# A graph network and a mixture of experts on one core: products up with all three parts in the same columns, GELU out of PSUM, and four reorderings

## The chip, the cores and the metric

The kernel runs on one NeuronCore of a Trainium2 chip. The metric is the time on the device in microseconds (us), the median of the runs shown. A profile is one execution recorded by the hardware; its times count from the start of the profiled span. The engines are TensorE (PE; PEld is its loading of weights), VectorE (DVE), ScalarE (ACT), GpSimd (POOL) and SyncE (SP), which issues plain DMAs.

## What is computed

A graph network on 1250 nodes of 512 features is added to its input, and then a mixture of 8 experts is added to that: each of the first 512 rows goes, normalised, through the two experts drawn for it, weighted.

```
x = x + gnn(layernorm(x))                 # two layers over 41250 edges, three decoder products
xf = layernorm(x)[:512]                   # the tokens of the experts
order = argsort(expert_indices.reshape(-1)); token_ids = order // 2
xg = xf[token_ids]
for e in range(8):
    h = gelu(xg @ w1[e], approximate=False)     # 512 -> 256
    y = where(bin_ids == e, h @ w2[e], y)       # 256 -> 512
x = x + zeros.at[token_ids].add(w * y)
```

(The edges are 20000 drawn pairs in both directions and a loop at each node. In the last line the sum has as many rows as there are tokens.)

## The kernel before

**Stages.** The adjacency matrix is built by TensorE from one-hot rows that VectorE makes (line 752). The two layers of the network are products of it with the features, cut into two or three bf16 parts (lines 1681, 1810, 1819). A decoder of three FP32 products follows (lines 1775, 1783, 1793), 128 rows a chunk for the last, ten chunks c. `sum_rows` (line 1082) adds a chunk's result to x. The first four chunks are the tokens; they are normalised and stored to `x2_rows` in HBM, from which each expert's rows are gathered.

**Routing.** Beside the first layer VectorE finds for each token and expert the slot it gets. An expert has 128 + 32 slots (`SLOTS` = 160, `MORE` = 32); the last 32 of four experts (a team, `TEAM` = 4) are gathered and scattered together, as `tail`. The scatter-adds of one token's two results must not be under way together. So an assignment is marked `late` (must be among an expert's last 32, the tails) or `early` (must be among the first 128), or is free. Late is a pair of neighbouring experts' second, early its first, and early is also the lower of two experts of one team. Before, lines 921 to 928 make these marks. `load` (lines 969 to 974) holds the fullest lists against their limits and chooses the sparse or a dense path; here the sparse one is taken, by all engines at the branch `sparse != 0`. `scale_sum1` (line 984) then scales the first layer's sums.

**Experts.** All products of the experts have both operands in two parts, hi and lo, each FP32 rounded to fp32r and its rest; of the four cross products the one of both rests is left out. Per expert e:

- TensorE transposes the gathered rows (`transpose_gathered`, 1859; `transpose_tails`, 1869). ScalarE takes the hi part out of PSUM (1406, 1411), VectorE the rest (1112, 1116).
- `up_slots` makes two halves m of the 256 hidden features, each in a bank of its own, 2 + m. Four products (line 1886) of w1's hi part with x's hi and lo lying side by side fill 320 columns, four (line 1889) of w1's rest with x's hi add to the first 160.
- ScalarE copies the right 160 columns out (`keep_part`, 1426), VectorE adds the left ones (`sum_hidden`, 1127). Only then may TensorE write the banks again. ScalarE makes the GELU (1444), a hi copy (1448) and the tails' GELU (1450); VectorE the rest (1150).
- `down_slots` (1848) gives 512 columns; VectorE scales them by the weight (`keep_results`, 1135). `down_tails` (1911) and `keep_tails` (1433) do the same for the tails of a team.
- ScalarE rounds the weights of expert e + 3 (`first_parts`, 1418), VectorE takes their rests (`up_rest`, 1060; `down_rest`, 1063). The weights of experts 0 and 1 are rounded by GpSimd (658), their rests are taken between additions (`weights_rest`, 1057).

TensorE's order is: up 0, then for each e up e + 1, transposes e + 2, down e; after experts 3 and 7 the tails' product.

**Scatter-adds.** GpSimd issues them (672) in the order of experts, the tails of team 0 after expert 3's, those of team 1 last. That of expert e waits until that of expert e − 2 has landed, and from expert 4 on until the first tails' has:

```
                    if e >= 2:
                        pool.wait_ge(s_added[e % 2], 16 * (e // 2))
                    if e >= TEAM:
                        pool.wait_ge(s_added_more, 16 * (e // TEAM))
```

The second tails' scatter-add waits for expert 6's. A scatter-add adds 128 rows to `out`; a slot that is free has a row of its own behind the tokens.

## Time and profile before

| | us |
|---|---|
| median of 3 runs | 169.47 |
| lowest, highest | 169.32, 170.09 |
| the profiled execution | 169.9 |
| its span | 168.1 |
| TensorE busy in it | 144.9 |
| VectorE busy in it | 130.9 |
| ScalarE, GpSimd busy in it | 90.9, 41.4 |

The granted clock of TensorE is full until its last product. The timeline puts like instructions in a row together: its start, its length, engine, line, operation, tiles and count, and in brackets how long the engine had been idle before it and who released it. A row of products is longer than the distance to the next row, since the end of one product overlaps the start of the next; the distances between starts tell what a group costs. Where two products are recorded for one FP32 product, the count is double.

### The profile page before, as it was taken

To read this page: it belongs to the slowest core of one execution; us is meant where nothing else is said; L and a number is where in the kernel's file an instruction comes from. 1 tells how busy PE (TensorE), PEld (TensorE's weight loads), DVE (VectorE), ACT (ScalarE), POOL (GpSimd) and SP (SyncE) were. 2 spreads that over 40 slices of the span, in tenths; PEclk is the share of its full clock that TensorE was granted. 3 is DMA by queue.
4 is the path that set the end of the run, shared out by engine and by line. 5 is a ranking of instruction groups with operands and counts; after the bars stand their busy time and mean duration, and the time that the engine had idled before them with its cause. 6 is when DMAs were issued, how large, how long until landed. Compare 5 with 4: busy or idle time off the path is not lost.

```text
span 168.1 us, 3574 instructions
## 1 busy us (share of the span) xinstructions
PE 144.9 (86%) x1146; PEld 99.4 (59%) x1149; DVE 130.9 (78%) x317; ACT 90.9 (54%) x224; POOL 41.4 (25%) x57
## 2 busy tenths in 40 slices
PE   2968899999999999989999999899968999987500
PEld 1446677888788757546735444445957886875100
DVE  1899999999999789996469388399759999895100
ACT  3278777777788784013314506903588896653100
POOL 8300000000000000000000900078204877618550
PEclk9999999999999999999999999999999999999975
DMA  4999999994000000000000003335890986543874
GB/s 90 324 350 254 349 375 368 366 364 166 4 0 4 6 0 6 0 0 4 0 0 0 4 0 125 125 101 159 275 388 15 191 170 101 95 66 48 107 106 62
DMA packets 15355, 21.72 MB, mean 129 GB/s; under 512 B 2942, under 2 KB 7808, under 8 KB 15332
## 3 DMA queue, kind: packets, MB, share of 16 engines
q1 hardware_dynamic: 12994, 16.02, 28.7%
q0 software_dynamic: 2240, 5.24, 17.6%
q8 instruction: 13, 0.21, 0.5%
q10 hardware_dynamic: 98, 0.17, 0.3%
q14 instruction: 10, 0.08, 0.2%
HBM read 15.19 MB, written 6.23 MB: 127 GB/s over the span
## 4 chain that ended last, share of the span: by engine, by line
PE 45%; DVE 26%; ACT 9%; issue 7%; DMA 6%; POOL 2%; POOLq 1%; DVEq 0%; ACTq 0%
DVE ring L752 11%; PE bank L1560 9%; PE bank L1793 7%; DMA out<-at,to_i 6%; PE bank L1535 4%; PE bank L1886 3%; PE bank L1681 3%; PE bank L1889 2%; PE bank L1481 2%; PE bank L1819 2%; PE bank L1525 2%; DVE stats L1088 2%; PE bank L1848 2%; DVE x_sb L1082 2%; DVE ring L900 2%
## 5 line engine op out<-in xcount | busy, mean ns | idle before, releaser
L1560 PE MATMUL bank<-ring 128*128 128x110 bf16 x324 | 30.0, 222 | 3.9 <-DVE ring L752 2.7
L752 DVE TENSOR_TENSOR ring<-iota_slots,lo 128x1024 bf16<-128x1024 f16 (+1 forms) x41 | 27.4, 669 | 0.0
L1560 PEld LDWEIGHTS bank<-ring 128*128 128x128 bf16 x324 | 19.7, 98 | 11.9 <-issue 5.9
L658 POOL CAST at_r<-ew 128x1024 fp32r<-128x1024 f32 x4 | 4.6, 1183 | 83.6 <-PE bank L1810 83.6
L1266 ACT CAST at<-bank 128x400 f32 (+1 forms) x41 | 20.6, 503 | 7.5 <-PE bank L1566 6.7
L752 DVE TENSOR_TENSOR ring<-iota_dst,key 128x880 bf16<-128x880 f16 (+1 forms) x41 | 24.4, 594 | 0.0
L672 POOL DMA_INDIRECT out<-at,to_i x10 | 19.0, 1898 | 19.8 <-DVE at L1135 8.8
L1793 PE MATMUL bank<-wd3t_sb,at 128*128 128x512 f32 x40 | 17.9, 598 | 0.7 <-ACT at L1365 0.7
L1681 PE MATMUL bank<-at,ring 128*128 128x512 bf16 (+1 forms) x89 | 16.7, 343 | 0.1
L661 POOL DMA_INDIRECT ring<-x_rows,from_i x10 | 12.7, 1269 | 15.5 <-DMA x_rows<-at 12.8
L1886 PE MATMUL bank<-xnt_r,at_r 128*128 128x320 f32 x64 | 12.9, 323 | 2.9 <-DVE ring L1127 2.6
L1793 PEld LDWEIGHTS bank<-wd3t_sb,at 128*128 128x128 f32 x40 | 7.4, 190 | 10.0 <-issue 8.1
L1886 PEld LDWEIGHTS bank<-xnt_r,at_r 128*128 128x128 f32 x64 | 9.5, 189 | 6.0 <-issue 5.1
L1848 PE MATMUL bank<-at_r 128*128 128x512 f32 x32 | 11.9, 414 | 1.2 <-DVE at_r L1150 1.2
L1681 PEld LDWEIGHTS bank<-at,ring 128*128 128x128 bf16 x90 | 8.7, 98 | 7.0
L1418 ACT CAST at_r<-ew 128x1024 fp32r<-128x1024 f32 x12 | 11.9, 1037 | 0.0
L1535 PE MATMUL bank<-w1c,xnt 128*128 128x129 f32 x80 | 11.4, 284 | 0.0
L1082 DVE TENSOR_TENSOR x_sb<-x_sb,bank 128x512 f32<-128x512 f32 x10 | 6.8, 684 | 5.8 <-PE bank L1793 5.7
L1535 PEld LDWEIGHTS bank<-w1c,xnt 128*128 128x128 f32 x80 | 9.8, 191 | 0.1
L1889 PE MATMUL bank<-xnt_r,ew_r 128*128 128x160 f32 x64 | 9.2, 266 | 0.0
L1406 ACT CAST xnt_r<-bank 128x256 fp32r<-128x256 f32 x16 | 5.1, 372 | 7.3 <-PE bank L1859 7.3
L1889 PEld LDWEIGHTS bank<-xnt_r,ew_r 128*128 128x128 f32 x64 | 8.9, 190 | 0.0
(226 smaller groups left out, 267.0 us busy)
## 6 DMA issues: line engine op xcount, KB each, us to landing
ew<-in_w SPq DMA_DIRECT2D x16, 512.0 KB, 9.5
x_sb<-in_x SPq DMA_DIRECT2D x9, 256.0 KB, 5.0
out<-x_sb SPq DMA_DIRECT2D x9, 256.0 KB, 4.4
wd3t_sb<-in_Wd3T SPq DMA_DIRECT2D x1, 512.0 KB, 5.3
x_rows<-xn SPq DMA_DIRECT2D x1, 512.0 KB, 2.8
x_rows<-at SPq DMA_DIRECT2D x1, 512.0 KB, 2.8
w1t_sb<-in_W1T SPq DMA_DIRECT2D x1, 256.0 KB, 4.5
bd_sb<-in_bd SPq DMA_DIRECT2D x1, 256.0 KB, 4.5
```

What stands on the lines that cost most here:

```text
L661: nc.gpsimd.indirect_dma_start(to, None, x2_rows, bass.IndirectOffsetOnAxis(from_i[:, i:i + 1].bitcast(mybir.dt.uint32), 0)).then_inc(gath ...
L672: nc.gpsimd.indirect_dma_start(out[0:T + 3 * P, :], bass.IndirectOffsetOnAxis(to_i[:, i:i + 1].bitcast(mybir.dt.uint32), 0), of, None, com ...
L752: last = v.tensor_tensor(hot[:, slot, 0:tiles].rearrange("p t (n a) -> p t n a", a=2), lanes[:, 0:n].rearrange("p (n a) -> p n a", a=2).un ...
L1266: nc.scalar.copy(at[:, :, bass.ds(column, wide)], bank[j][:, 0:CH * wide].rearrange("p (c n) -> p c n", c=CH)).then_inc(s_placed, 1)
L1418: nc.scalar.copy(hi, w).then_inc(s_whi_act, 1)
L1535: last = mm(bank[6][:, 0:HID + 1], xnt[:, k, c * P:(c + 1) * P], w1c[:, k], start=(k == 0), stop=(k == KD - 1))
L1560: last = mm(to, hot_src[:, j, t], hot_dst[:, j, t], start=(t == 0 and not ends), stop=(first and t == tiles - 1), skip_group_check=not ends)
L1681: last = mm(bank[4 + i][:, 0:n], parts[k][:, s], at[:, s, a:a + n], start=(k == 0 and s == 0), stop=(k == last_k and s == CH - 1))
L1793: last = mm(bank[4 + c % 4][:, 0:D], y2t[:, k, c * P:(c + 1) * P], wd3t_sb[:, k], start=(k == 0), stop=(k == 1))
L1848: last = mm(acc, lhs(a, k), rhs(b, k), start=(i == 0), stop=(i == len(passes) - 1))
L1886: mm(acc[:, 0:2 * SLOTS], w1_hi[:, k, m * P:(m + 1) * P], xg_t[:, e % 2, k].rearrange("p h t -> p (h t)"), start=(k == 0), stop=False)
L1889: last = mm(acc[:, 0:SLOTS], w1_lo[:, e, k, m * P:(m + 1) * P], xg_t[:, e % 2, k, 0], start=False, stop=(k == KD - 1))
```

## The change

Six things are changed.

1. **Products up**: the hi and lo parts of x now meet w1's hi part in two products of 160 columns, one after the other, that add into the same columns as the third part. Both halves m lie in one bank, and experts take the banks 2 and 3 in turn. TensorE waits for the GELU of expert e − 2 instead of for `sum_hidden`.
2. **GELU from PSUM**: `keep_part` and `sum_hidden` are gone, and ScalarE's GELU reads the bank.
3. **Additions**: with `FREE` = 6 only the scatter-adds of experts 6 and 7 wait for the first tails'. For that, in team 0 the lower of a pair is also early where the other expert is 4 or 5, so the marks are made in another way, with one step fewer.
4. **Weights**: the rests of experts 0 and 1 are taken one by one after chunks 3 to 6, and that of expert 2's w1 before chunk 8.
5. **Decoder**: the first activation of the second span goes ahead of the second square root, and `decode3` waits for each of its two input halves by itself.
6. **Scaling**: the first `scale_sum1` goes ahead of the comparison of loads.

```diff
@@ add_to_tokens
-                    if e >= TEAM:
+                    if e >= FREE:            # FREE = TEAM + 2
                         pool.wait_ge(s_added_more, 16 * (e // TEAM))
@@ routing marks
-            for i, k in enumerate((0, 1, 0)):
-                v.scalar_tensor_tensor(in_turn[:, :, i], gif[:, :, 1 - k], 1.0, gif[:, :, k], ALU.add, ALU.is_equal)
+            for k in range(TOPK):
+                v.scalar_tensor_tensor(in_turn[:, :, k], gif[:, :, 1 - k], 1.0, gif[:, :, k], ALU.add, ALU.is_equal)
...
-            late, early = in_turn[:, :, 0:TOPK], in_turn[:, :, 1:TOPK + 1]
-            v.tensor_scalar(team[:, :, :], gif[:, :, :], float(TEAM), None, ALU.is_ge)
+            v.tensor_scalar(team[:, :, :], gif[:, :, :], float(TEAM), float(NE - FREE), ALU.is_ge, ALU.mult)
             for k in range(TOPK):
                 last = v.tensor_tensor(below[:, :, k], gif[:, :, k], gif[:, :, 1 - k], ALU.is_lt)
             link(last)
-            link(v.tensor_tensor(one_team[:, :], team[:, :, 0], team[:, :, 1], ALU.is_equal))
-            link(v.tensor_tensor(below[:, :, :], below[:, :, :], one_team[:, :].unsqueeze(2).to_broadcast([P, TC, TOPK]), ALU.mult))
-            link(v.tensor_tensor(below[:, :, :], below[:, :, :], early, ALU.max))
-            early = below[:, :, :]
+            for k in range(TOPK):
+                last = v.scalar_tensor_tensor(team[:, :, k], team[:, :, k], float(FREE), gif[:, :, 1 - k], ALU.add, ALU.is_gt)
+            link(last)
+            link(v.tensor_tensor(below[:, :, :], below[:, :, :], team[:, :, :], ALU.mult))
+            late, early = in_turn[:, :, 0:TOPK], below[:, :, :]
@@ VectorE, weights and chunks
-            for c in range(CH - 1):
+            for c in range(CH - 3):
                 sum_rows(c)
...
-                if c == TC + 1:
-                    weights_rest(0)
-                if c == TC + 3:
-                    weights_rest(1)
+                if c >= TC - 1:
+                    weight_rest_of(*divmod(c - TC + 1, 2))
...
+                sum_rows(CH - 3)
+                dve.wait_ge(s_whi_act, 2)
+                up_rest(2)
+                sum_rows(CH - 2)
                 dve.wait_ge(s_slot_weight, 1)
                 gathered_rest(0)
                 sum_rows(CH - 1)
                 gathered_rest(1)
-                sum_hidden(0)
                 for e in range(NE):
-                    if e + 2 < NE:
+                    if 1 <= e < NE - 2:
                         dve.wait_ge(s_whi_act, 2 * (e + 1))
                         up_rest(e + 2)
...
-                    if e + 1 < NE:
-                        sum_hidden(e + 1)
@@ ScalarE
             finish_y1(2)
+            finish_y2(1, (0,))
             take_deviations(1)
-            finish_y2(1)
+            finish_y2(1, (1,))
             finish_y2(2)
...
-                    act.wait_ge(s_hs_sum, KF * (e + 1))
-                    nc.scalar.activation(hs_raw[:, :, 0:P], hs_raw[:, :, 0:P], ACT.Gelu).then_inc(s_gelu_sp, 1)
+                    act.wait_ge(s_up_sp, KF * (e + 1))
+                    if e >= 1:
+                        act.wait_ge(s_hs_lo, e)
+                    nc.scalar.activation(hs_raw, of_up(e)[:, :, 0:P], ACT.Gelu).then_inc(s_gelu_sp, 1)
...
-                    if e + 1 < NE:
-                        keep_part(e + 1)
@@ TensorE
             def decode3(c):
-                pe.wait_ge(s_y2, 2 * (c * P // 512) + 2)
...
                 for k in range(2):
+                    pe.wait_ge(s_y2, 2 * (c * P // 512) + k + 1)
@@ up_slots;  of_up(e) = bank[2 + e % 2][:, 0:KF * SLOTS] as [p, m, t]
+                    if e >= 2:
+                        pe.wait_ge(s_hs_tail, e - 1)
                     for m in range(KF):
-                        if e >= 1:
-                            pe.wait_ge(s_hs_sum, KF * (e - 1) + m + 1)
-                        acc = bank[2 + m]
+                        acc = of_up(e)[:, m]
+                        rows = [xg_t[:, e % 2, k] for k in range(KD)]
                         for k in range(KD):
-                            mm(acc[:, 0:2 * SLOTS], w1_hi[:, k, m * P:(m + 1) * P],
-                               xg_t[:, e % 2, k].rearrange("p h t -> p (h t)"), start=(k == 0), stop=False)
+                            for h in range(2):
+                                mm(acc, w1_hi[:, k, m * P:(m + 1) * P], rows[k][:, h], start=(k == 0 and h == 0), stop=False)
                         for k in range(KD):
-                            last = mm(acc[:, 0:SLOTS], w1_lo[:, e, k, m * P:(m + 1) * P], xg_t[:, e % 2, k, 0],
-                                      start=False, stop=(k == KD - 1))
+                            last = mm(acc, w1_lo[:, e, k, m * P:(m + 1) * P], rows[k][:, 0], start=False, stop=(k == KD - 1))
```

The scaling's move is shown by the order. Three places follow as the engines have their instructions in a row, before and after; bank numbers are kept.

TensorE, product up of expert 2 and the transposes of expert 3 behind it (xnt_r holds the gathered rows, at_r and ew1_r the parts of w1). Before:

```order
L1886 MATMUL bank2<-xnt_r,at_r 128x320 x4
L1889 MATMUL bank2<-xnt_r,ew1_r 128x160 x4
L1886 MATMUL bank3<-xnt_r,at_r 128x320 x4
L1889 MATMUL bank3<-xnt_r,ew1_r 128x160 x4
L1859 MATMUL bank0<-ident,ring 128x128 x2
L1859 MATMUL bank1<-ident,ring 128x128 x2
```

After:

```order
L1869 MATMUL bank2<-xnt_r,at_r 128x160 x8
L1871 MATMUL bank2<-xnt_r,ew1_r 128x160 x4
L1869 MATMUL bank2<-xnt_r,at_r 128x160 x8
L1871 MATMUL bank2<-xnt_r,ew1_r 128x160 x4
L1842 MATMUL bank0<-ident,ring 128x128 x2
L1842 MATMUL bank1<-ident,ring 128x128 x2
```

The wide products have become twice as many narrow ones, and both halves go to bank 2 where they had bank 2 and bank 3.

VectorE after the slots' one-hots (`ring<-iota_slots,rank`), with the comparison of loads (`load`, `path_i`), the scaling of the first sums (`xnt<-bank4,xnt`) and the bias additions (`x_sb<-x_sb,bd3_sb`). Before:

```order
L968 TENSOR_SCALAR ring<-iota_slots,rank 128x256 x8
L969 TENSOR_REDUCE load<-loads 128x3
L970 TENSOR_SCALAR load<-load 128x1
L971 SCALAR_TENSOR_TENSOR load<-load 128x1
L972 SCALAR_TENSOR_TENSOR load<-load 128x1
L973 CAST path_i<-load 1x1
L974 TENSOR_SCALAR path_i<-load 1x1
L984 TENSOR_TENSOR xnt<-bank4,xnt 128x512
L1008 TENSOR_TENSOR x_sb<-x_sb,bd3_sb 128x512 x3
```

After:

```order
L968 TENSOR_SCALAR ring<-iota_slots,rank 128x256 x8
L975 TENSOR_TENSOR xnt<-bank4,xnt 128x512
L1002 TENSOR_REDUCE load<-loads 128x3
L1003 TENSOR_SCALAR load<-load 128x1
L1004 SCALAR_TENSOR_TENSOR load<-load 128x1
L1005 SCALAR_TENSOR_TENSOR load<-load 128x1
L1006 CAST path_i<-load 1x1
L1007 TENSOR_SCALAR path_i<-load 1x1
L999 TENSOR_TENSOR x_sb<-x_sb,bd3_sb 128x512 x3
```

The scaling stands ahead of the six instructions of the loads, which now stand between it and the bias additions.

ScalarE in the decoder, from the first square root of the normalisation (`rstd<-mv,eps`) on; `at2<-bank0,bd2_sb` is the first half of the second span's activations. Before:

```order
L1387 ACTIVATE rstd<-mv,eps 128x2
L1369 ACTIVATE xn<-x_sb,rstd 128x512 x2
L1359 ACTIVATE at2<-bank3,bd1_sb 128x256
L1387 ACTIVATE rstd<-mv,eps 128x2
L1365 ACTIVATE at2<-bank0,bd2_sb 128x512
L1365 ACTIVATE at2<-bank1,bd2_sb 128x512
L1365 ACTIVATE at2<-bank2,bd2_sb 128x256
L1365 ACTIVATE at2<-bank3,bd2_sb 128x256
```

After:

```order
L1378 ACTIVATE rstd<-mv,eps 128x2
L1360 ACTIVATE xn<-x_sb,rstd 128x512 x2
L1350 ACTIVATE at2<-bank3,bd1_sb 128x256
L1356 ACTIVATE at2<-bank0,bd2_sb 128x512
L1378 ACTIVATE rstd<-mv,eps 128x2
L1356 ACTIVATE at2<-bank1,bd2_sb 128x512
L1356 ACTIVATE at2<-bank2,bd2_sb 128x256
L1356 ACTIVATE at2<-bank3,bd2_sb 128x256
```

The first half has moved ahead of the second square root.

## Rows read from the trace of the kernel before

**Rows 1.** Waits of TensorE: engine, line, releaser, total, times, longest.

```profile
PE bank L1886 <- DVE ring L1127: 2.6, 4, 1.3
PE bank L1848 <- DVE at_r L1150: 1.2, 1, 1.2
PE bank L1793 <- ACT at L1365: 0.7, 1, 0.7
PE bank L1714 <- ACT xnt L1328: 0.6, 1, 0.6
PE bank L1722 <- DVE chosen_kind L933: 0.3, 1, 0.3
```

**Rows 2.** Timeline of VectorE, routing: start, length, engine, line, operation, tiles.

```profile
65.96 0.16 DVE L925 TENSOR_TENSOR one_team<-team 128x4 f32<-128x4 f32 x1
...
66.57 0.17 DVE L929 TENSOR_TENSOR paired<-in_turn,below 128x8 f32<-128x8 f32 x1
...
72.64 0.17 DVE L969 TENSOR_REDUCE load<-loads 128x3 f32<-128x24 f32 x1
...
73.56 0.67 DVE L984 TENSOR_TENSOR xnt<-bank,xnt 128x512 f32<-128x512 f32 x1
```

**Rows 3.** Timelines of TensorE, then ScalarE, where the decoder waits.

```profile
102.08 2.74 PE L1783 MATMUL bank<-at,wd2t_sb 128*128 128x512 f32 x8
105.52 8.85 PE L1793 MATMUL bank<-wd3t_sb,at 128*128 128x512 f32 x20 [0.71 <-ACT at L1365]
...
104.02 0.29 ACT L1387 ACTIVATE rstd<-mv,eps 128x2 f32<-128x2 f32 x1 [1.20 <-DVE mv L1089]
```

**Rows 4.** Timeline of TensorE in the expert stage.

```profile
117.74 0.82 PE L1886 MATMUL bank<-xnt_r,at_r 128*128 128x320 f32 x4 [0.22 <-issue]
...
125.27 0.82 PE L1886 MATMUL bank<-xnt_r,at_r 128*128 128x320 f32 x4 [1.32 <-DVE ring L1127]
...
126.33 0.79 PE L1886 MATMUL bank<-xnt_r,at_r 128*128 128x320 f32 x4
126.96 0.58 PE L1889 MATMUL bank<-xnt_r,ew_r 128*128 128x160 f32 x4
127.37 0.61 PE L1859 MATMUL bank<-ident,ring 128*128 128x128 f32 x4
127.73 0.48 PE L1848 MATMUL bank<-at_r 128*128 128x512 f32 x1
...
137.04 0.47 PE L1848 MATMUL bank<-at_r 128*128 128x512 f32 x1
...
138.61 1.92 PE L1911 MATMUL bank<-ew,ring 128*32 128x512 f32 x16
140.46 0.85 PE L1886 MATMUL bank<-xnt_r,at_r 128*128 128x320 f32 x4
...
151.52 0.43 PE L1848 MATMUL bank<-at_r 128*128 128x512 f32 x1
```

**Rows 5.** Timeline of VectorE in the expert stage.

```profile
129.46 0.55 DVE L1127 TENSOR_TENSOR ring<-bank,ring 128x160 f32<-128x160 f32 x2
129.92 1.22 DVE L1060 TENSOR_TENSOR ew_r<-ew,at_r 128x1024 fp32r<-128x1024 f32 x1
...
134.11 0.55 DVE L1127 TENSOR_TENSOR ring<-bank,ring 128x160 f32<-128x160 f32 x2
...
153.14 0.75 DVE L1135 TENSOR_SCALAR at<-bank,slot_weight 128x512 f32<-128x512 f32 x1 [0.70 <-PE bank L1848]
```

**Rows 6.** Timeline of GpSimd at the end.

```profile
151.18 2.21 POOL L672 DMA_INDIRECT out<-at,to_i  x1 [3.70 <-DMA out<-at,to_i]
...
156.68 1.55 POOL L672 DMA_INDIRECT out<-at,to_i  x1 [1.43 <-DMA out<-at,to_i]
...
162.22 1.55 POOL L672 DMA_INDIRECT out<-at,to_i  x1 [1.65 <-DMA out<-at,to_i]
```

**Rows 7.** Chain of waits before the first tails' scatter-add: start, length, what.

```profile
144.93 0.75 issue
```

61 lines of the change are left out of this document (24 added, 37 removed).

## The prediction

> **What bounds the kernel now.** I read the waits of TensorE first, then the timeline of the expert stage, then the chain of waits to its end. Times are microseconds from the start of the profiled span, which is 168.1 long in a run of 169.9; the median of the runs shown is 169.47. I work out changes of the span and take them off the median, because run and median differ by something that the change doesn't touch.
>
> TensorE has few waits [rows 1]: 0.3 for the routing masks, 0.6 for the first scaled hidden features, 0.7 for ScalarE's decoder activations, 2.6 in four pieces for VectorE's addition at line 1127, 1.2 ahead of the last product down. In the expert stage VectorE has no idle time between 129.46 and 134.66: its additions of line 1127 come round every 134.11 − 129.46 = 4.65 [rows 5], so it paces the experts. TensorE's own round is shorter: product up 125.27 to 127.37 = 2.10, transposes 0.36, product down 137.04 to 138.61 = 1.57, together 4.03 [rows 4]. Behind the products hangs a second chain, on GpSimd: the scatter-add of expert 4 starts at 151.18, after 3.70 idle for the landing of the first tails' scatter-add; that of expert 6 follows at 156.68, when expert 4's has landed; the second tails' follows at 162.22, when expert 6's has; the span ends 5.88 after that [rows 6]. This chain, and not TensorE's last product, ends the kernel.
>
> **The change part by part.** *Routing and additions.* A pair of experts of one token now counts as ordered by the first 128 slots up to expert 5, so experts 4 and 5 no longer wait for the first tails (line 680). The masks take one dependent step less: two of the steps between 65.96 and 66.57, 0.20 each, give way to one of two short instructions, and one of line 914's three instructions goes [rows 2]. I take 0.2 of TensorE's 0.3 [rows 1]; the bounds are 0 and 0.3.
>
> *Scaling.* The first scaling of line 984 is moved ahead of six small instructions that take from 72.64 to 73.56 = 0.92 [rows 2]. TensorE waited 0.6 for it, so 0.6 is gained and the rest is slack. The six now stand between it and three bias additions, and the path flags come some 0.6 later; both have followers that wait for TensorE further on, so I cost them at nothing. Behind this point everything is one chain, so 0.2 + 0.6 = 0.8 goes through to the end. The bounds are 0.5 and 0.9.
>
> *Decoder.* The first activation of the second span is put ahead of the second square root on ScalarE, which until 104.02 waited 1.20 for VectorE [rows 3]. Its input is ready about 103: decode2's first product, two records, starts at 102.08, and a record of this width takes 8.85 ÷ 20 = 0.44 in decode3 [rows 3]. So it fits in a hole of ScalarE, delays no square root, and TensorE can start decode3 without its wait, 0.71 at 105.52 [rows 3]. The bounds are 0 and 0.71, since the first gather could be the next thing late. It is an issue of GpSimd that this edit doesn't bring forward. The rows show no wait of TensorE for a gather, so its slack isn't visible; I take the full 0.71.
>
> *Weights.* The four rests of experts 0 and 1 go one by one into holes that VectorE had between additions, and the rest of expert 2's weights goes ahead of the loop. The work is the same. It gives VectorE the start of the stage free; alone it gains nothing on TensorE's chain. I cost it at 0, bounds −0.2 and 0.2.
>
> *Products up.* Before, an expert had for each half of its hidden features four products of 320 columns and four of 160. Now it has twelve of 160, all into one bank per expert, taken in turns. Four of 320 take 126.33 to 126.96 = 0.63, that is 0.158 a product; four of 160 take 126.96 to 127.37 = 0.41, that is 0.103 [rows 4]. Halving the columns doesn't halve the time, since a weight load stands before each product and the order of the kernel keeps 24 of these where there were 16. So each expert's product up grows by 2 × (8 × 0.103 − 0.63) = 0.40, to 2.50. The bounds are 2.10, were the columns alone to count, and 3.35, were each new product to cost what a wide one does. I take 0.103, because its row has the new shape exactly.
>
> By the Trainium skill, TensorE: Matmul & The Clock Gate, section LDWEIGHTS, a load takes its columns divided by 1.2, an estimate of 107 ns for 128 columns, and no fast load is made for FP32. The trace agrees, with 103 where the stream is shorter than the load; by the page's figure the product up would be 2.56 instead of 2.50.
>
> *What VectorE and ScalarE lose.* VectorE loses the two additions, 129.46 to 129.92 = 0.46 [rows 5], and its round becomes 4.19. ScalarE loses the two copies out of PSUM. TensorE's round is now 2.50 + 0.36 + 1.57 = 4.43 and sets the pace. With two banks in turn it waits only for the GELU of two experts back, long done, so the waits at line 1886 go.
>
> **The stage, added up** in the old trace's time with the decoder's 0.71 taken off first. Up 0 starts at 117.74 − 0.71 = 117.03 [rows 4], up 1 at 119.53 and ends at 122.03. Transposes and down 0 take 1.93; up 2 starts at 123.96 (before: 125.27). Up 3 is 4.43 later, at 128.39; up 4 at 133.22, with 0.40 more for the tails' transposes; up 5 at 139.50, with 1.85 more for the first tails' product (138.61 to 140.46, [rows 4]); up 6 at 143.93; up 7 at 148.36, ending at 150.86. Before, down 6 started at 151.52 [rows 4]. So TensorE is 0.66 ahead, less than the decoder's 0.71: eight times 0.40 paid eats all that the waits give back. The rewritten products earn nothing by themselves.
>
> **The end.** From the start of down 6 to its scaled result it is 153.14 + 0.75 − 151.52 = 2.37 [rows 4, 5]; a result reaches GpSimd's scatter 0.75 later, as the chain shows at 144.93 [rows 7]. So expert 6's scatter-add could start at 150.86 + 2.37 + 0.75 = 153.98. Expert 4's must have landed: its result is ready about 145.3, it starts about 146.7 behind the first tails', and lands 5.5 later (from 151.18 to 156.68) at 152.2, in time. Then 5.54 to the second tails' and 5.88 to the end [rows 6]: 165.4. With the 0.8 of the first two parts the span is 164.6, that is 3.5 less than 168.1. Of this 3.5 most is not TensorE's work but the wait of the scatter-adds that is gone: 156.68 becomes 153.98. **Forecast: 169.47 − 3.5 = 166.0.** Its own range is 165.3 to 166.9: the decoder's gain lost to the gather gives 166.7, the small ends of routing and scaling 166.3, a landing 0.5 quicker 165.5.
>
> **Rivals.** *Cheap halves.* Both halves of x meet the same weights; were the second load hidden, a product of 160 columns would cost half a wide one, 0.079, and the product up stay at 2.10. Then VectorE's 4.19 paces, up 7 ends near 148.1 and the result is 163.3. For it speaks that the two loads are of equal contents; against it that the trace counts as many loads as products and that 0.103 was paid by every narrow product. The same page's section Back-to-back issue gap gives 81 ns for a pair of load and product at 128 columns, which would lead here too; the trace has more, 103 at 160 columns. Chance 0.08.
>
> *Dear halves*, the one that ends slower. If writing the same columns again back to back makes each new product as long as a wide one, 0.158, the product up is 3.35, 0.85 over my figure, and eight of them move the end by 6.8, to 172.8. It decides from a price of 0.103 + 3.5 ÷ (8 × 16) = 0.130 a product. Against it: the four products of line 1889 write the same columns back to back already. Chance 0.05.
>
> *Round unchanged.* Transposes, casts, rests and the next product up form a loop through three engines, beside down's 1.57. If it, or VectorE, keeps the round at 4.65, four rounds lose 0.22 each: 166.9. For it speaks that VectorE's 4.19 leaves only 0.24. Chance 0.13.
>
> *Scatter-adds slower together.* The first tails' and experts 4 and 5 now overlap in the same DMA engines, beside the last stores. If the last two landings take 0.9 longer each, 167.8. Chance 0.10, half of it beyond 168.6.
>
> *The change doesn't do what it says.* More rows would have to go to the first slots than fit, and the slow dense path be taken. Counting the drawn indices by the new rule gives at most 88 of 128 ordered early, 21 of 32 late and 142 of 160 in all, so it isn't taken; I give it nothing.
>
> **Chances.** Forecast 0.64, cheap halves 0.08, round unchanged 0.13, scatter-adds 0.10, dear halves 0.05. A measurement here can tell about 0.5%, so faster means below 168.6: 0.64 + 0.08 + 0.13 + 0.05 = 0.90. Within 0.5% 0.05, slower 0.05. The range 163.6 to 168.2 leaves out the dear halves, most of the cheap ones and the slower half of the scatter case.
>
> **What would show it.** Four narrow products spaced 0.41 in both groups of the product up; rounds of 4.4 with no wait of TensorE at its head; VectorE idle some 0.2 a round; no wait of TensorE before decode3's fifth chunk and before the hidden features' product; expert 4's scatter-add starting right behind the first tails', and 5.5 between expert 6's and the second tails'. I am wrong if the narrow products are spaced otherwise, if expert 6's scatter-add waits for a landing, or if TensorE waits for the first gather.

## The result, and the profile after

| | median us | lowest, highest | ratio to before, 95% interval |
|---|---|---|---|
| before, 5 runs | 169.71 | 169.32, 170.09 | |
| after, 5 runs | 168.15 | 167.80, 168.45 | 0.9909, 0.9889 to 0.9929 |

The change makes the kernel faster by 1.56 us. Forecast was 3.5. The direction was right, the size was not. The time lies just inside the stated range of 163.6 to 168.2, but outside the forecast's own, 165.3 to 166.9.

The page of after, its first part: busy time, share of the span and instructions of each engine.

```profile
span 166.1 us, 3648 instructions
## 1 busy us (share of the span) xinstructions
PE 147.8 (89%) x1210; PEld 104.0 (63%) x1213; DVE 126.7 (76%) x300; ACT 87.1 (52%) x208; POOL 42.5 (26%) x57
```

TensorE is busy 2.9 more than before, VectorE 4.2 less and ScalarE 3.8 less: work went where it was meant to go. The waits of TensorE in after (line, releaser, total, times, longest), to hold against [rows 1]:

```profile
PE bank L1831 <- DVE at_r L1142: 1.2, 1, 1.2
PE bank L1842 <- DMA ring<-x_rows,from_i: 1.0, 2, 0.5
```

The waits of 2.6, 0.7, 0.6 and 0.3 have gone, as forecast. A new one has come, for the gathered rows. The timeline of TensorE in after, from the end of the build of the adjacency matrix on, shows where the time goes (start, length, engine, line, operation, tiles, and the idle time ahead in brackets):

```profile
57.33 0.16 PE L1571 MATMUL bank<-zeros_bf,ident_bf 128*128 128x2 bf16 x1
...
93.14 3.17 PE L1776 MATMUL bank<-wd3t_sb,at 128*128 128x512 f32 x7
...
112.29 0.66 PE L1842 MATMUL bank<-ident,ring 128*128 128x128 f32 x4 [0.52 <-DMA ring<-x_rows,from_i]
...
115.61 0.66 PE L1842 MATMUL bank<-ident,ring 128*128 128x128 f32 x4 [0.51 <-DMA ring<-x_rows,from_i]
116.02 1.10 PE L1869 MATMUL bank<-xnt_r,at_r 128*128 128x160 f32 x8
...
123.37 1.09 PE L1869 MATMUL bank<-xnt_r,at_r 128*128 128x160 f32 x8
124.30 0.61 PE L1871 MATMUL bank<-xnt_r,ew_r 128*128 128x160 f32 x4
124.74 1.06 PE L1869 MATMUL bank<-xnt_r,at_r 128*128 128x160 f32 x8
125.64 0.61 PE L1871 MATMUL bank<-xnt_r,ew_r 128*128 128x160 f32 x4
126.09 0.61 PE L1842 MATMUL bank<-ident,ring 128*128 128x128 f32 x4
...
128.03 1.09 PE L1869 MATMUL bank<-xnt_r,at_r 128*128 128x160 f32 x8
...
151.54 0.43 PE L1831 MATMUL bank<-at_r 128*128 128x512 f32 x1
```

Up 0 starts 1.72 earlier than in [rows 4] (116.02 against 117.74), and down 6 starts at 151.54 as before at 151.52. The whole lead is lost on the way. One round is 128.03 − 123.37 = 4.66, what it was before (4.65), but now TensorE is never idle in it. The product up takes 126.09 − 123.37 = 2.72. Eight narrow products (160 columns) take 125.64 − 124.74 = 0.90 and four take 126.09 − 125.64 = 0.45: 0.112 each.

VectorE, which paced the rounds in [rows 5], has 0.45 idle in each (timeline of VectorE in after):

```profile
126.97 0.76 DVE L1112 TENSOR_TENSOR xnt_r<-bank,xnt_r 128x256 fp32r<-128x256 f32 x2 [0.45 <-ACT xnt_r L1398]
...
131.63 0.76 DVE L1112 TENSOR_TENSOR xnt_r<-bank,xnt_r 128x256 fp32r<-128x256 f32 x2 [0.45 <-ACT xnt_r L1398]
```

The timeline of GpSimd at the end of after, to hold against [rows 6]: the first tails' scatter-add, then those of experts 4 to 7 and of the second tails.

```profile
144.90 1.74 POOL L672 DMA_INDIRECT out<-at,to_i  x1 [2.66 <-ACT at L1417]
146.94 1.80 POOL L672 DMA_INDIRECT out<-at,to_i  x1 [0.30 <-issue]
150.45 2.13 POOL L672 DMA_INDIRECT out<-at,to_i  x1 [1.71 <-DVE at L1124]
154.70 1.55 POOL L672 DMA_INDIRECT out<-at,to_i  x1 [2.13 <-DVE at L1124]
157.54 1.55 POOL L672 DMA_INDIRECT out<-at,to_i  x1 [1.29 <-DVE at L1124]
160.38 1.55 POOL L672 DMA_INDIRECT out<-at,to_i  x1 [1.29 <-DMA out<-at,to_i]
```

Expert 4's stands right behind the first tails' (146.94), and expert 6's waits for its own result, not for a landing. This is as forecast.

To add up, one more pair of rows of before is wanted, the end of the build stage and the start of the last decoder product:

```profile
57.72 0.16 PE L1588 MATMUL bank<-zeros_bf,ident_bf 128*128 128x2 bf16 x1
...
94.67 1.55 PE L1793 MATMUL bank<-wd3t_sb,at 128*128 128x512 f32 x3
```

| stretch | before | after | difference | forecast |
|---|---|---|---|---|
| start to the end of the build | 57.72 | 57.33 | −0.39 | 0 |
| to the last decoder product | 36.95 | 35.81 | −1.14 | −0.80 |
| to up 0 | 23.07 | 22.88 | −0.19 | −0.71 |
| to down 6 | 33.78 | 35.52 | +1.74 | +0.05 |
| to expert 6's scatter-add | 5.16 | 3.16 | −2.00 | −2.04 |
| to the second tails' | 5.54 | 5.68 | +0.14 | 0 |
| to the end | 5.88 | 5.72 | −0.16 | 0 |
| sum | 168.1 | 166.1 | −2.00 | −3.50 |

The first row isn't of the change: over the fourteen traces of this study the build ends anywhere from 57.28 to 58.23. (The two at 58.23, e2 and e11, have a mean granted clock of 0.83 from 10 to 20, where after has 1.00.) Without it the sum is −1.61, close to the measured 1.56. The row of +0.14, the landing of expert 6's scatter-add, is one execution's and varies much; see the last section.

### The profile page after: what moved, and what is told of

Its sections match the earlier page's. It is cut to its first block, busy times and chain, and to the rows that moved or that the text cites. A ratio compares the mean times of both kernels' runs of the same rounds, so it can differ in the third digit from the quotient of the medians.

```text
span 166.1 us, 3648 instructions
## 1 busy us (share of the span) xinstructions
PE 147.8 (89%) x1210; PEld 104.0 (63%) x1213; DVE 126.7 (76%) x300; ACT 87.1 (52%) x208; POOL 42.5 (26%) x57
## 4 chain that ended last, share of the span: by engine, by line
PE 58%; DVE 24%; DMA 6%; issue 5%; POOL 3%; ACT 1%; POOLq 1%; DVEq 0%; SPq 0%
DVE ring L752 13%; PE bank L1664 10%; PE bank L1869 9%; PE bank L1543 8%; PE bank L1831 7%; PE bank L1871 4%; PE bank L1518 4%; DMA ring<-x_rows,from_i 2%; PE bank L1842 2%; POOL ring L661 2%; PE bank L1802 2%; DVE stats L1090 2%; DVE x_sb L1084 2%; DMA at<-in_src 2%; DMA x_rows<-at 2%
## 5 line engine op out<-in xcount | busy, mean ns | idle before, releaser
L661 POOL DMA_INDIRECT ring<-x_rows,from_i x10 | 13.5, 1350 | 15.3 <-DMA x_rows<-at 12.6
L1869 PE MATMUL bank<-xnt_r,at_r 128*128 128x160 f32 x128 | 17.1, 277 | 0.0
L1869 PEld LDWEIGHTS bank<-xnt_r,at_r 128*128 128x128 f32 x128 | 15.6, 192 | 2.3 <-issue 1.4
L1112 DVE TENSOR_TENSOR xnt_r<-bank,xnt_r 128x256 fp32r<-128x256 f32 x16 | 6.0, 419 | 7.0 <-ACT xnt_r L1398 7.0
L1871 PE MATMUL bank<-xnt_r,ew_r 128*128 128x160 f32 x64 | 9.8, 275 | 0.0
L1124 DVE TENSOR_SCALAR at<-bank,slot_weight 128x512 f32<-128x512 f32 x8 | 6.0, 747 | 4.0 <-PE bank L1831 4.0
```

The source lines that it names most:

```text
L661: nc.gpsimd.indirect_dma_start(to, None, x2_rows, bass.IndirectOffsetOnAxis(from_i[:, i:i + 1].bitcast(mybir.dt.uint32), 0)).then_inc(gath ...
L1869: mm(acc, w1_hi[:, k, m * P:(m + 1) * P], rows[k][:, h], start=(k == 0 and h == 0), stop=False)
L1871: last = mm(acc, w1_lo[:, e, k, m * P:(m + 1) * P], rows[k][:, 0], start=False, stop=(k == KD - 1))
```

## The experiments

My theory after this reading: (1) a product of 160 columns costs the load of its weights, 0.112, and eight more of them for four wide ones lengthen the stage; (2) the decoder's gain is lost to a gather that GpSimd now issues more slowly; (3) the four reorderings are right. The rivals stand in each expectation. All numbers of stretches below are taken from the traces as in the table above, counted from the end of the build. Each run was timed beside before, whose median was 169.24 to 169.66 there; so the ratios compare, and the times only roughly. In time, e1, e5, e6, e7, e9, e10, e11 and e12 came out above the range of my first theory (A), e4 below it; e8 is within its range by the ratio alone.

### The two halves of the change apart

`e1_reorder_only` keeps the four reorderings and has the products up, `keep_part` and `sum_hidden` of before:

```diff
-                        for k in range(KD):
-                            for h in range(2):
-                                mm(acc, w1_hi[:, k, m * P:(m + 1) * P], rows[k][:, h], start=(k == 0 and h == 0), stop=False)
+                        for k in range(KD):
+                            mm(acc[:, 0:2 * SLOTS], w1_hi[:, k, m * P:(m + 1) * P],
+                               xg_t[:, e % 2, k].rearrange("p h t -> p (h t)"), start=(k == 0), stop=False)
```

> The four reorderings with the products up, the copy and the addition of the kernel before. My theory after the result: the narrow products cost TensorE 0.112 each, 2.67 an expert, and not 2.50, so that eight products up cost more than the waits gave back. From the start of the first product up to the end of the last it was 33.8 before and is 35.5 in the changed kernel; here it should be 33.8 or a little less, with VectorE's round of 4.65 and a wait of TensorE at the third product up. So it should beat the changed kernel by some 1.5: 166.4 to 166.9. Rival: the products with the GELU from PSUM are worth what they seem to be, and this one is slower than the changed kernel, 168.5 to 169.

Measured: 167.37, ratio 0.9898 (0.9869 to 0.9928). `e2_products_only` is the opposite: before with the new products and the GELU from PSUM alone.

> The kernel before with the products up and the GELU from PSUM alone. My theory: the stage grows by 1.7 (8 x 0.57 more in the products, less the waits), but the end waited for the landing of the first tails' scatter-add anyway, so half is hidden: 169.7 to 170.5, no gain over the kernel before. Rival: the waits given back outweigh it, 168.5.

Measured: 169.97, ratio 1.0041 (1.0024 to 1.0057), slower than before. The whole gain comes from the reorderings; the products alone lose 0.7, with rounds of 4.67 too. In e1 the stretch from up 0 to down 6 is 34.01, in e2 35.49, in after 35.52, before 33.78. In e2 that costs 1.71 in the stage. From down 6 to the second tails' it is 9.30 instead of 10.70. Of these 1.40, 0.81 lie ahead of expert 6's scatter-add (4.35 instead of 5.16), which waited for a landing anyway; the other 0.59 is a shorter landing behind it (4.95 instead of 5.54), which one execution can't tell from chance. So 1.71 − 0.81 = 0.90 is left, near the 0.7 of the medians: the loss is smaller than the stage shows. On top of the reorderings the products cost 1.4 in the traces (span less build: 107.35 in e1, 108.77 in after; e1's profiled execution, 166.86, is the fastest of its six), but only 0.0011 of the ratio, 0.2 us, in the medians, whose intervals leave room for anything from 0.7 in the products' favour to 1.0 against them. So that the products lose is measured where they stand alone, and only likely where the reorderings stand beside them.

### The reorderings, undone one by one

```diff
 e3_no_weights
-                if c >= TC - 1:
-                    weight_rest_of(*divmod(c - TC + 1, 2))
+                if c == TC + 1:
+                    weights_rest(0)
+                if c == TC + 3:
+                    weights_rest(1)
 e4_no_additions
-                    if e >= FREE:
+                    if e >= TEAM:
 e5_no_decoder
-            finish_y2(1, (0,))
             take_deviations(1)
-            finish_y2(1, (1,))
+            finish_y2(1)
 e6_no_scaling
-            scale_sum1(0)
             route(v.tensor_reduce(load[:, 0:KINDS], loads[:, :, :], AX.X, ALU.max))
...
+            scale_sum1(0)
```

(e3 also puts the rest of expert 2's w1 back into the loop of experts. e4 also has the routing marks of before, e5 the wait of `decode3` for both halves.)

> The changed kernel without the reordering of the weights' rests. Theory that VectorE, kept busy in its holes, slows GpSimd's issuing of the gathers: the first three issues go back from 1.95, 1.24, 1.41 to about 1.2, 1.0, 0.9, TensorE's two waits for gathered rows (1.0 together) go, but the rests come later on VectorE, so the time is within 0.4 of the changed kernel. Rival: the issues have the same lengths with and without, the waits stay, and the time is the same or 0.3 longer.

> The changed kernel with the additions undone: experts 4 and 5 wait for the first tails' scatter-add again, and the marks are made in the old way. My theory: expert 4's goes about 150.5 instead of 146.9, expert 6's waits for it until about 156, the end is 1.2 later: 169.2 to 169.5. Rival: with TensorE as late as it is, the wait is hidden and the time stays 168.2.

> The kernel after, with the decoder put back: its second half starts only when both products it reads are done, as before. Theory A (the decoder's gain is eaten): in the trace of after the decoder reorder saves about 0.7 to 1.0 us, but TensorE then waits 0.52 and 0.51 us for the first gathered rows, whose issue by GpSimd has become longer. Undone, the decoder costs its 0.7 us again and these two waits shrink by about as much: time within 0.3 us of after (168.15). Theory B (it is kept): +0.7 us, 168.7 to 169.0, with the gather waits as long as in after.

> The kernel after, with the scaling put back: VectorE takes the loads and the choice of the path ahead of the scaling of the first layer's sums, as before. Theory A (the term of 0.6 us of the prediction): TensorE waits again for VectorE ahead of the hidden-feature products, 0.5 to 0.6 us, and the time is 168.6 to 168.9, 0.5 to 0.7 above after. Theory B: in after the products behind the scaling start 1.34 us earlier than before, of which the additions alone account for part, and something else (the choice of the path, that GpSimd and SyncE use later) now comes later, so that less is lost: 168.2 to 168.4.

| undone | median | ratio (interval) | against after by ratio, us | which stretch, us |
|---|---|---|---|---|
| weights | 167.87 | 0.9917 (0.9889 to 0.9945) | +0.1 | none by over 0.4 |
| additions | 168.91 | 0.9983 (0.9966 to 1.0001) | +1.3 | to the decoder +0.20, down 6 to expert 6's scatter-add +1.09 |
| decoder | 168.91 | 0.9960 (0.9940 to 0.9979) | +0.9 | to up 0 +0.18 |
| scaling | 169.07 | 0.9989 (0.9975 to 1.0003) | +1.4 | to the decoder +0.85 |

Each undone edit brings its own wait back: the waits of TensorE in e5 and in e6 have one of these lines each,

```profile
PE bank L1775 <- ACT at L1356: 0.7, 1, 0.7
```

```profile
PE bank L1700 <- ACT xnt L1322: 0.6, 1, 0.6
```

and in the timeline of GpSimd in e4 the scatter-adds of experts 4 and 6 wait for landings again:

```profile
151.49 1.74 POOL L672 DMA_INDIRECT out<-at,to_i  x1 [4.19 <-DMA out<-at,to_i]
...
156.45 1.55 POOL L672 DMA_INDIRECT out<-at,to_i  x1 [1.36 <-DMA out<-at,to_i]
```

So in the changed kernel the additions' edit brings expert 6's scatter-add 1.09 forward (3.16 behind down 6 instead of 4.25), and not the whole 2.00 of the table: before's 5.16 shrinks by 0.91 without it, because TensorE comes later to a landing that doesn't. Behind it e4's landing took 4.75 where after's took 5.68, so that in these two traces the second tails' gains only 0.16.

The weights' edit is worth nothing that the medians show, as costed. Scaling is worth more than the 0.6 of its wait: the stretch grows by 0.85. Of it 0.57 is the wait, 0.16 more lies between the start of the row of products ahead and that of the hidden features' (7.20 in e6, 6.47 in after), and these products then take 0.95 instead of 0.84. On the decoder I have to take half of my theory back. I expected its gain to be eaten whole; the medians say that 0.9 is lost without it (0.2 to 1.5 by the ends of the intervals), the traces 0.18 up to up 0. The three single losses come to 3.5, more than the 1.7 that all four edits are worth together in e1. After's own ratio is in each of the three, and the last landing differs from trace to trace (6.14 in e5, 5.68 in after; see the end of the document). So how much of the decoder's gain arrives stays open between 0.2 and 0.9.

### What a narrow product costs

`e7_short_products` cuts all but the first product of each half to 96 columns. It leaves out eleven of the twelve terms of columns 96 to 159.

```diff
-                                mm(acc, w1_hi[:, k, m * P:(m + 1) * P], rows[k][:, h], start=(k == 0 and h == 0), stop=False)
+                                n = SLOTS if k == 0 and h == 0 else 96
+                                mm(acc[:, 0:n], w1_hi[:, k, m * P:(m + 1) * P], rows[k][:, h, 0:n], start=(k == 0 and h == 0), stop=False)
...
-                            last = mm(acc, w1_lo[:, e, k, m * P:(m + 1) * P], rows[k][:, 0], start=False, stop=(k == KD - 1))
+                            last = mm(acc[:, 0:96], w1_lo[:, e, k, m * P:(m + 1) * P], rows[k][:, 0, 0:96], start=False, stop=(k == KD - 1))
```

> The kernel after, but eleven of the twelve products up of each half stream only 96 of their 160 columns (the sums of columns 96 to 159 lack those eleven terms; the first product of each half stays 160 wide). Theory A (a product whose weights change every time is paced by the load of its weights, 0.112 us in after, not by its columns): the spacing stays at 0.107 to 0.113 us, a half still takes about 1.3 us, and the time is within 0.3 us of after, 167.8 to 168.4. Theory B (paced by its columns): 0.067 a product, up takes about 1.75 us instead of 2.70, the round falls until VectorE paces it, about 4.2, and the time is 3 us less, about 165.

Measured: 168.71, ratio 0.9940 (0.9924 to 0.9955). A half in its timeline of TensorE:

```profile
117.64 1.06 PE L1870 MATMUL bank<-xnt_r,at_r 128*128 128x160 f32 x8
118.53 0.61 PE L1872 MATMUL bank<-xnt_r,ew_r 128*128 128x96 f32 x4
118.98 1.06 PE L1870 MATMUL bank<-xnt_r,at_r 128*128 128x160 f32 x8
```

118.98 − 117.64 = 1.34, with 96 columns as with 160. Columns don't set this price. (The row of eight is named by its first, wide member.) Nor does it come from adding into the same columns again: the transposes of [rows 4], 128 columns each into columns of their own, start at 127.37, 127.49, 127.60 and 127.71, 0.11 apart as well. What all of these have in common is a load of 128 columns of weights. That the time is even 0.3% above after has a reason of its own in the profiled execution, in a table of stretches (length, busy time of PE, PEld, DVE, ACT and POOL, then the granted clock, DMA share, GB/s):

```profile
121.00:126.00 5.00, 5.00 (x27) 4.48 (x27) 2.83 (x6) 3.80 (x9) 0.00 (x0) 0.66 0.81 311
```

The granted clock is 0.66 there, part of the stretch at 1.2 GHz instead of 2.4; in the 5 us before TensorE had been busy throughout with narrow products, and in after, where it had too, the clock stayed full. The stage of this execution is 1.36 longer than after's (36.88). The other five runs hardly had such a dip, with mean granted clocks of 0.980 to 0.990 against 0.973 here (after: 0.987 to 0.991), and still took 168.37 to 168.87; what is left of the 0.3% isn't explained.

`e8_old_in_turn` is e1 with its wide and narrow products in turns instead of four and four.

```diff
                         for k in range(KD):
                             mm(acc[:, 0:2 * SLOTS], w1_hi[:, k, m * P:(m + 1) * P],
                                xg_t[:, e % 2, k].rearrange("p h t -> p (h t)"), start=(k == 0), stop=False)
-                        for k in range(KD):
                             last = mm(acc[:, 0:SLOTS], w1_lo[:, e, k, m * P:(m + 1) * P], xg_t[:, e % 2, k, 0],
                                       start=False, stop=(k == KD - 1))
```

> The four reorderings with the products up of before, but the four wide products (320 columns) and the four narrow ones (160) of a half alternate instead of standing in two groups. Theory A (the load of weights costs about 0.11 us and hides only under a wide product's stream): every narrow product's load now lies under a wide stream, each pair takes about 0.22 us, a half about 0.88 against 1.04 grouped (0.63 + 0.41), up 1.8 against 2.08; VectorE's 4.65 us still paces the round, so the time stays within 0.4 us of the reorderings alone (167.37) and TensorE idles 0.3 us longer a round. Theory B (narrow products are paced by their columns): no change in the 2.08, and none in the time.

Measured: 167.95, ratio 0.9891 (0.9867 to 0.9914), as e1. Its timeline of TensorE:

```profile
116.75 0.35 PE L1892 MATMUL bank<-xnt_r,at_r 128*128 128x320 f32 x1
116.93 0.24 PE L1894 MATMUL bank<-xnt_r,ew_r 128*128 128x160 f32 x1
117.01 0.35 PE L1892 MATMUL bank<-xnt_r,at_r 128*128 128x320 f32 x1
```

My 0.22 for a pair was wrong, and with it theory A in this form: it is 117.01 − 116.75 = 0.26, four of them 1.04, exactly the 0.63 + 0.41 of the grouped order [rows 4]. A narrow product behind a wide one follows it after 0.18 and is itself followed after 0.08. I read it so: its own load was hidden under the wide stream, but it is too short to hide the next one's. Then each narrow product leaves part of the next load bare, whatever the order, and a run of narrow ones costs 0.112 each. The steps are measured, the overlap behind them is my reading. Now [rows 4] reads differently. The group of four narrow products in it, asked for in narrower windows of the timeline of TensorE before, is

```profile
126.96 0.24 PE L1889 MATMUL bank<-xnt_r,ew_r 128*128 128x160 f32 x1
127.03 0.50 PE L1889 MATMUL bank<-xnt_r,ew_r 128*128 128x160 f32 x3
```

so 0.41 for four was one of 0.07 and three of 0.11 (127.37 − 127.03 = 0.34). The mean of 0.103 is the mean of a group with a wide product ahead of it. The new kernel has no such product left: 24 × 0.112 = 2.69 against 2.72 in the trace, where I forecast 2.50.

By the Trainium skill, TensorE: Matmul & The Clock Gate, section LDWEIGHTS, the load's time goes by its 128 columns, an estimate of 107 ns. The trace agrees in kind, and has 112; e7 shows that what is streamed doesn't count (96 or 160 columns).

### What drew out the gathers

In after the first three gathers' issues take 1.95, 1.24 and 1.41 (timeline of GpSimd), and VectorE's rests of weights run beside them (timeline of VectorE):

```profile
107.87 1.95 POOL L661 DMA_INDIRECT ring<-x_rows,from_i  x1 [12.59 <-DMA x_rows<-at]
110.12 1.24 POOL L661 DMA_INDIRECT ring<-x_rows,from_i  x1 [0.30 <-issue]
111.67 1.41 POOL L661 DMA_INDIRECT ring<-x_rows,from_i  x1 [0.31 <-issue]
```

```profile
107.57 1.22 DVE L1054 TENSOR_TENSOR ew_r<-ew,at_r 128x1024 fp32r<-128x1024 f32 x1
108.71 0.68 DVE L1084 TENSOR_TENSOR x_sb<-x_sb,bank 128x512 f32<-128x512 f32 x1
109.30 1.22 DVE L1054 TENSOR_TENSOR xnt_r<-ew,at_r 128x1024 fp32r<-128x1024 f32 x1
```

`e10_psum_rests` takes the first operand of the rests of experts 0 and 1 (but the first rest) and of expert 2's w1 from PSUM, in two halves; these rests then hold other values. (Ahead of them it also waits for ScalarE's last activation of the decoder, since the bank is in use until then; the rests stand where they stood, the first of them at 105.77 against 105.84 in after.)

```diff
-                v.tensor_tensor(lo, weights(e)[i], weights_hi(e)[i].bitcast(F32), ALU.subtract).then_inc(s_wlo, 1)
+                v.tensor_tensor(lo[:, 0:half], bank[2][:, 0:half], weights_hi(e)[i].bitcast(F32)[:, 0:half], ALU.subtract)
+                v.tensor_tensor(lo[:, half:], bank[2][:, 0:half], weights_hi(e)[i].bitcast(F32)[:, half:], ALU.subtract).then_inc(s_wlo, 1)
```

> The kernel after, but the lower parts of the weights of experts 0 and 1 (all but the first of the four) and of one of expert 2 are taken from PSUM: VectorE subtracts from a PSUM bank in two halves of 512 columns instead of from SBUF in one of 1024, so these lower parts hold other values. The time of VectorE is nearly the same (2 x 0.69 against 1.22 us), but its first operand is no longer in SBUF. Theory A (GpSimd's issue of an indirect transfer is drawn out by VectorE's operations with all operands in SBUF): the first three issues of gathered rows take about 0.95 to 1.2 us each instead of 1.95, 1.24 and 1.41, TensorE's two waits for gathered rows (0.52, 0.51) go, the first product up starts 0.5 to 1.0 us earlier and the time falls by 0.4 to 1.0 from after, 167.2 to 167.8. Theory B (the issues take as long as they take because of the traffic of the weights and the queue, 255 to 300 GB/s at that point): issues and waits as in after, time as after or 0.1 to 0.3 more.

Its timelines of GpSimd and, for two of the rests, of VectorE:

```profile
108.19 1.17 POOL L661 DMA_INDIRECT ring<-x_rows,from_i  x1 [12.96 <-DMA x_rows<-at]
109.66 0.97 POOL L661 DMA_INDIRECT ring<-x_rows,from_i  x1 [0.30 <-issue]
110.93 0.94 POOL L661 DMA_INDIRECT ring<-x_rows,from_i  x1 [0.30 <-issue]
...
108.17 0.68 DVE L1060 TENSOR_TENSOR ew_r<-bank,at_r 128x512 fp32r<-128x512 f32 x1
...
109.36 0.68 DVE L1059 TENSOR_TENSOR xnt_r<-bank,at_r 128x512 fp32r<-128x512 f32 x1
```

Theory A holds for the mechanism. The rests run beside the issues as in after, yet the issues fall to 1.17, 0.97 and 0.94, TensorE waits for no gather, and from the last decoder product to up 0 it takes 22.32 instead of 22.88: 0.75 less than before's 23.07, the 0.71 that I had forecast for the decoder. The time doesn't follow: 167.89, above my 167.2 to 167.8, ratio 0.9915 (0.9899 to 0.9930) against after's 0.9909. In the profiled execution expert 6's scatter-add starts 0.64 earlier (154.06) and the second tails' 0.04 (160.34), the landing between them having taken 0.60 longer. One execution can't tell whether that is chance, but by the medians too little of the 0.56 gained up to up 0 arrives.

### A mixed version

If narrow products are dear and VectorE has 0.45 to spare, half of the trade is better than all of it. `e9_mixed` keeps the narrow products for the first half of the hidden columns and takes wide ones for the second, whose part ScalarE copies and VectorE adds back in PSUM.

```diff
+                    acc = bank[2 + e % 2][:, SLOTS:3 * SLOTS]
+                    for k in range(KD):
+                        mm(acc, w1_hi[:, k, P:2 * P], rows[k].rearrange("p h t -> p (h t)"), start=(k == 0), stop=False)
...
+                    v.tensor_tensor(of_up(e)[:, 1], of_up(e)[:, 1], hs_part, ALU.add).then_inc(s_hs_sum, 1)
```

> The kernel after, but only the first half of the hidden columns is added up in the same columns of PSUM; the second half has wide products again (320 columns, 8 instead of 12), whose second part ScalarE copies (160 columns) and VectorE adds back in PSUM. TensorE's up falls from 2.70 to about 1.34 + 1.04 = 2.38, its round from 4.66 to about 4.35; VectorE's round gains one addition of 160 columns, 4.19 + 0.25 = about 4.45. Theory A (each round is the longer of the two engines' sums): round about 4.45, seven rounds save 1.4 us, time 166.3 to 166.9. Theory B (the added hand-overs TensorE, ScalarE, VectorE, ScalarE lengthen the chain within the round): round 4.65 or more, time 167.9 to 168.6.

Measured: 167.32, ratio 0.9859 (0.9839 to 0.9878): 0.85 us below after, the lowest of the study, though e1's interval touches its own. A round of TensorE in e9:

```profile
124.34 1.10 PE L1889 MATMUL bank<-xnt_r,at_r 128*128 128x160 f32 x8 [1.13 <-issue]
125.28 0.61 PE L1891 MATMUL bank<-xnt_r,ew_r 128*128 128x160 f32 x4
125.72 0.79 PE L1895 MATMUL bank<-xnt_r,at_r 128*128 128x320 f32 x4
126.35 0.57 PE L1897 MATMUL bank<-xnt_r,ew_r 128*128 128x160 f32 x4
...
128.70 1.09 PE L1889 MATMUL bank<-xnt_r,at_r 128*128 128x160 f32 x8
```

The round is 128.70 − 124.34 = 4.36, with VectorE full, and the stage 34.27 instead of 35.52: theory A has the round, not the time. Ahead of this round stands a wait of 1.13. `e11_rows_first` has ScalarE take expert 2's rows ahead of the copies of expert 3's weights, and `e12_both_first` also expert 1's second part (the line `keep_part(1)` is in e12 alone), which VectorE then also adds ahead of expert 2's rests of x:

```diff
+                    if e == 0:
+                        keep_part(1)
+                        keep_gathered(e + 2)
                     if e + 3 < NE:
                         first_parts(e + 3)
```

> The version of mixed products (first half narrow, second half wide), with ScalarE taking the gathered rows of expert 2 ahead of the two copies of expert 3's weights (1.99 us). In the mixed version TensorE waits 1.13 us ahead of expert 2's products, because VectorE waits 1.86 for ScalarE's copy of these rows, which stands behind the weights. Theory A: the wait goes, up of expert 2 starts 1.0 to 1.2 earlier, the rounds stay at 4.36 and the last scatter-adds start earlier by what the tails and their landings allow: 166.2 to 166.9 against 167.32. Theory B: VectorE, which has no idle time left in these rounds, or the landing of the scatter-adds, which the tails share one destination with, gives the wait back later: 167.1 to 167.5.

> The mixed version with both engines changed once, in the first round: ScalarE takes expert 1's second part and then expert 2's gathered rows ahead of the two copies of expert 3's weights, and VectorE adds expert 1's part ahead of expert 2's rests. In the version with only the rows taken first, TensorE's wait of 1.13 went, but VectorE waited 1.57 for expert 1's part, which still stood behind the weights, and its rounds of 4.36 started no earlier (first addition for expert 1 66.75 after the end of the build stage, against 66.45 in the mixed version). Theory A (VectorE's chain of rounds, full from there on, sets the end): that addition now comes about 2.5 us earlier, the rounds start 0.5 to 1.0 earlier, and so does the last product up (93.13 after the end of the build stage in the mixed version): time 166.3 to 166.9, ratio to before 0.981 to 0.985. Theory B (something else in the first rounds, as the GELU of expert 1 behind the weight copies, or the weights themselves, holds the chain): time as the mixed version, ratio 0.985 to 0.988.

Measured: 167.77, ratio 0.9906 (0.9875 to 0.9936), and 167.68, ratio 0.9882 (0.9849 to 0.9914): neither better than e9. The wait of 1.13 went each time, one of 0.4 came a round later, and VectorE's moved on. Timelines of VectorE, first e11, then e12:

```profile
124.98 0.33 DVE L1125 TENSOR_TENSOR bank<-bank,ring 128x160 f32<-128x160 f32 x1 [1.57 <-ACT ring L1428]
```

```profile
124.39 1.23 DVE L1065 TENSOR_TENSOR ew_r<-ew,at_r 128x1024 fp32r<-128x1024 f32 x1 [1.38 <-ACT at_r L1423]
```

In e12 VectorE waits for the copies of expert 3's weights themselves, and starts its full rounds at 124.39, as it did in e9 (the builds end at 57.72 and 57.71); down 6 starts in e12 and e9 34.32 and 34.27 after up 0. ScalarE's two copies of weights are the bound of the first round, which is theory B of the last experiment.

## Why the prediction was off

- **Bound of the kernel now, end of the kernel**: right. The end was forecast at −2.04 and gave −2.00, by the mechanism named: expert 4's scatter-add behind the first tails', expert 6's waiting for its own result. e4 has the landings' waits back. But only 1.09 of it is the edit's by e4; 0.91 is part of the longer stage, hidden in before's wait.
- **Products up: the step that failed.** "I take 0.103, because its row has the new shape exactly." The shape was the same and the neighbours were not. The price is 0.112, and 24 × 0.009 = 0.22 more per expert is 2.72 instead of 2.50, a round of 4.66 instead of 4.43, and 1.76 over eight experts, where the stage measured 1.69 over the forecast (+1.74 instead of +0.05). The figure of the Trainium skill, which I set beside the row and didn't use, gave 2.56 and was nearer. The bound of 3.35 held. The number was in the trace of before: had I asked what stood ahead of each of the four, 0.07 and three of 0.11 would have come out.
- **Round unchanged** came true in its number, 4.66, but not in its mechanism: VectorE idles 0.45 per round, and TensorE paces. My price for it was low as well, since all eight products up are longer and not four rounds.
- **Decoder**: taken at its upper end of 0.71, got 0.19 in the trace. I had named the gather as what could be late next and then not costed it, since the rows showed no wait. What I missed is that VectorE's rests hold up GpSimd's issues. In before they met the fourth one (1.89 at 113.55), which TensorE needs only later. With the decoder earlier they meet the first ones, with the weights' edit (after) or without it: in e3 the issues take 1.72, 0.97 and 1.67, and TensorE waits 0.5 for the gathers. With the weights' edit and the old decoder, in e5, the first three take 1.16, 1.04 and 1.40, and TensorE waits for none. Taken out of the way altogether, in e10, the meeting gone gives the 0.7 back as far as up 0, though not in the time.
- **Routing and scaling**: forecast 0.8, got 1.14 in after; undone they cost 0.20 and 0.85. The wait of 0.6 was a lower bound.
- **Weights, GELU from PSUM**: right in their numbers (undone, the weights' edit costs 0.1); VectorE's round would be 4.66 − 0.45 = 4.21, forecast 4.19.
- **Dear halves, cheap halves**: neither. The price lies at 0.112, below the 0.130 from which the whole change would lose (the products alone lose at 0.112 already, in e2), and e7 excludes that columns count.
- **Scatter-adds slower together**: in part, and more than the table shows. After's +0.14 is the smallest of eleven: in the ten other traces with the additions' edit the last landing takes 5.85 to 6.71, against 4.75 to 5.54 in the three without it. After's median is 0.26 above its profiled execution.
- **The change doesn't do what it says**: it does; the gathers and scatter-adds of the sparse path stand in the timeline.
- **The range** of 163.6 to 168.2 covered the time by luck: its upper part was kept for slower scatter-adds, and what used it up was a longer stage.

Added up: 3.50 − 1.69 (stage) − 0.52 (decoder) + 0.34 (routing and scaling) − 0.04 (end) + 0.02 (the last two rows) = 1.61 in the traces, and 1.56 was measured. The sum is of one profiled execution each; that it meets the medians so closely is in part chance, as the landing shows.

## What to carry to other kernels

The mean price of a short product holds only in the company in which it was measured: by the reading above, a product whose stream is shorter than the next load pays for that load (0.112 here), so count the short products, not the columns, and look at what stands ahead of the first of a group. When an engine is relieved and another loaded, ask whether a part of the trade does better: half of it was worth 0.85 us more here than the whole (though not clearly more than none of it, e1). And a step moved into another engine's idle time can still hold up a third one that shares a resource with it, as the rests held up the gathers.

## What the runs showed of the hardware

GpSimd's issue of an indirect transfer waits for the end of VectorE's running instruction where that one reads both operands from SBUF, and takes its usual time after that. The usual time is 1.17 for the first issue and 0.94 to 0.97 for the next (e10). In after, VectorE's rest of 107.57 gives way to the next instruction at 108.71, so the issue of 107.87 should take 0.84 + 1.17 = 2.01; it took 1.95. The one of 110.12 meets a rest that ends at 109.30 + 1.14 = 110.44: 0.32 + 0.95 = 1.27, and it took 1.24. The same sum meets the others: in e3 the issue of 108.27 falls into a rest that gives way at 108.87, 0.60 + 1.17 = 1.77 against 1.72; in before the one of 113.55 into a rest that gives way at 114.54, 0.99 + 0.95 = 1.94 against 1.89. A rest that starts while an issue runs holds neither up (timelines of GpSimd and VectorE before):

```profile
109.51 1.17 POOL L661 DMA_INDIRECT ring<-x_rows,from_i  x1 [12.78 <-DMA x_rows<-at]
...
109.94 1.22 DVE L1057 TENSOR_TENSOR ew_r<-ew,at_r 128x1024 fp32r<-128x1024 f32 x1
```

Additions with one operand in PSUM don't hold an issue. By the Trainium skill, SBUF — State Buffer, section SBUF: two separate sides, VectorE with two SBUF inputs and a GpSimd operation that reads SBUF exclude each other for a whole instruction. The trace agrees in one direction, the issue that waits out the rest; in the other it doesn't show it, as the two rows above overlap at their usual lengths. e10 shows that a PSUM operand lifts it.

The landing of the last scatter-adds is the least steady part: from expert 6's to the second tails' it took 4.75 to 6.71 in fourteen traces (4.75 and 4.95 where expert 7's was issued 2.3 behind it, 5.68 to 6.71 with 2.8 in the others but before, which has 5.54 with 2.3). The three short ones are the three kernels in which experts 4 and 5 still wait for the first tails' landing, which speaks for the additions' edit lengthening this landing. Through what it would do so is not shown: no run here separates the spacing from the number of scatter-adds under way. A gain of 0.5 ahead of it can vanish in one profile; only the medians tell.
